# Expert stage of a state-space and mixture-of-experts layer: all gathers ahead of all scatters, rows kept in place, four weight buffers

## What is computed

```
gate = softmax(xr @ Wg); idx = argmax(gate); g = gate[idx]
loc  = rank of the token among those of its expert;  valid = loc < 256
dispatched[idx, loc] = xr                        # 16 x 256 x 128
h = relu(dispatched @ w1[e])                     # 256 x 128 @ 128 x 512
expert_out = h @ w2[e]                           # 256 x 512 @ 512 x 128
out = x + expert_out[idx, loc] * g * valid
```

## Time and profile before

| | |
|---|---|
| median of three runs | 721.25 us (720.04 to 721.40) |
| the profiled execution | span 721.6 us, 12778 instructions |
| TensorE products busy | 613.1 us, 85% |
| TensorE weight loads busy | 478.9 us, 66% |
| VectorE busy | 557.2 us, 77% |
| ScalarE busy | 527.8 us, 73% |
| GpSimd busy | 591.7 us, 82% |
| data moved | 85.20 MB, mean 118 GB/s |
| first gather starts | 616.30 us |
| last scatter's instruction ends | 716.10 us |

### The profile page before, as it was taken

One profiled execution on the slowest core, in us unless ns is written; L12 is line 12 of the kernel. 1 busy time (PEld: TensorE's weight loads), 2 busy tenths in 40 slices (PEclk: granted clock), 3 DMA queues, 4 the chain that ended last, 5 costly groups with the idle time before them and its releaser, 6 DMA issues.

```text
span 721.6 us, 12778 instructions
## 1 busy us (share of the span) xinstructions
PE 613.1 (85%) x4034; PEld 478.9 (66%) x4034; DVE 557.2 (77%) x892; ACT 527.8 (73%) x1043; POOL 591.7 (82%) x411
## 2 busy tenths in 40 slices
PE   5689989989989898998989999899878881987593
PEld 3336677757767776776767667676777761876483
DVE  5558899999999999999999999999987876222131
ACT  3699989899989989998999999899786320132130
POOL 5268999999999999999999999998997830656754
PEclk9989999999999999999999999999968895789897
DMA  4241533245145334524534442262343013345451
GB/s 138 82 149 62 155 111 131 86 129 170 64 150 164 127 106 121 157 84 128 180 110 133 105 171 77 75 207 84 115 127 113 23 42 98 88 149 163 122 176 50
DMA packets 60752, 85.20 MB, mean 118 GB/s; under 512 B 14321, under 2 KB 40214, under 8 KB 60686
## 3 DMA queue, kind: packets, MB, share of 16 engines
q1 hardware_dynamic: 57176, 78.05, 34.8%
q0 software_dynamic: 2560, 6.08, 2.8%
q10 hardware_dynamic: 950, 0.27, 0.2%
HBM read 72.27 MB, written 12.32 MB: 117 GB/s over the span
## 4 chain that ended last, share of the span: by engine, by line
POOL 55%; issue 21%; PE 13%; another core or an unknown queue 3%; DVE 3%; ACT 1%; DMA 1%; POOLq 1%; SPq 0%; DVEq 0%; ACTq 0%
POOL h L888 27%; POOL h L902 18%; PE ps L622 3%; POOL u L875 3%; PE ps L635 3%; POOL cs L913 2%; POOL fac L918 2%; PE ps L1676 1%; PE ps L1792 1%; POOL lnp L849 1%; POOL rstd L925 1%; PE ps L642 1%; PE ps L602 1%; PE ps L610 1%
## 5 line engine op out<-in xcount | busy, mean ns | idle before, releaser
L1413 DVE TENSOR_TENSOR_SCAN h<-ps,h 128x902 f32<-128x902 f32 x204 | 319.8, 1608 | 24.6 <-ACT ps L1029 16.5
L888 POOL TENSOR_TENSOR h<-u,scr 128x1280 f32<-128x1280 f32 x104 | 283.4, 2742 | 2.9
L1792 PEld LDWEIGHTS ps<-h,ident 128*128 128x128 f32 x1632 | 233.6, 196 | 22.9 <-issue 19.1
L1792 PE MATMUL ps<-h,ident 128*128 128x160 f32 x1632 | 239.9, 307 | 3.4 <-issue 3.4
L1139 ACT ACTIVATE z<-dtb,asc 128x240 f32<-128x240 f32 (+3 forms) x432 | 201.6, 537 | 0.1
L1029 ACT ACTIVATE ps<-z 128x820 f32<-128x820 f32 (+1 forms) x208 | 137.8, 687 | 35.5 <-DVE h L1413 28.9
L902 POOL TENSOR_TENSOR h<-h,scr 128x1280 f32<-128x1280 f32 (+1 forms) x52 | 138.0, 2654 | 0.7 <-DVE h L1429 0.7
L1464 DVE TENSOR_TENSOR h<-h,ps 128x640 f32<-128x640 f32 (+1 forms) x155 | 87.8, 577 | 0.2
L1676 PE MATMUL ps<-xnT,wT 128*128 128x488 f32 x144 | 73.9, 626 | 0.0
L1039 ACT ACTIVATE sqb<-h 128x208 f32<-128x208 f32 x102 | 44.8, 441 | 24.8 <-DVE h L1413 22.0
L398 POOL DMA_INDIRECT z<-rows_d,gidx x32 | 33.0, 1032 | 34.6 <-DVE gidx L532 25.2
(11 more groups left out here) (200 smaller groups left out, 801.4 us busy)
## 6 DMA issues: line engine op xcount, KB each, us to landing
scr<-b_d SPq DMA_DIRECT2D x52, 640.0 KB, 4.8
scr<-c_d SPq DMA_DIRECT2D x52, 320.0 KB, 4.9
z<-in_L_ffn_w_dram SPq DMA_DIRECT2D x32, 256.0 KB
cdg<-cdg_d SPq DMA_DIRECT2D x52, 60.0 KB
xx_d<-xx SPq DMA_DIRECT2D x8, 256.0 KB, 2.0
xxr<-xx_d SPq DMA_DIRECT2D x8, 256.0 KB, 2.8
rows_d<-h2b SPq DMA_DIRECT2D x16, 120.0 KB, 2.1
rows_d<-xxr SPq DMA_DIRECT2D x16, 120.0 KB, 2.3
```

The source lines that it names most:

```text
L888: pool.tensor_tensor(hr[:, hf * RH:(hf + 1) * RH, 1:SLOT].rearrange("p (n b) t -> p n b t", b=B), us.unsqueeze(1).to_broadcast([P, NST, B, ...
L1413: dve.tensor_tensor_scan(hs, region(G)[:, 0:(r1 - r0) * SLOT], hs, 0.0, ALU.mult, ALU.add).then_inc(gscan, 1)
L1792: pe.matmul(ps[:, YB, 0:H * BS], ident[:], hr[:, :, n * B:(n + 1) * B, 0:SEG], start=(n == 0), stop=False)
```

## The change

- `xs` has a place for each of the 16 experts, so no gather waits for a place. All 32 gathers are issued first, then all 32 scatters, each pair after its `fin_made`.
- `xin`, `xxe` and `fin` are gone, and with them `take_in` and `keep_xx` on ScalarE. TensorE turns the normed half straight from `xs`, after the gather. `take_out` reads the residual half of `xs`, writes its result over it, and the scatter reads it there. VectorE waits for the gather in place of `xxe_ready`, and no more for scatters.
- w1 and w2 have four places each. Four experts are loaded at the start; then w1 of e + 4 after the up products of e, w2 of e + 4 after the down products of e.
- To make room in `z`, the tiles `ohhi`, `idw`, `gtw` and `xTs` move from `z` into the area of `h`.
- The gathers have a semaphore for each expert, the scatters one for all. The loops over the experts are plain ones with the same order on TensorE and VectorE.

The diff, cut to its core:

```diff
-        w1s, o = take(z, o, 2, F)
-        w2s, o = take(z, o, 2, FC, DM)
-        xin, o = take(z, o, 2, CT, DM)
+        xs, o = take(z, o, E, CT, 2 * DM)
+        w1s, o = take(z, o, WR, F)
+        w2s, o = take(z, o, WR, FC, DM)
...
+        hTs, o = take(hf_, 0, 2, FC, CAP)
+        xTs, o = take(hf_, o, 2, CAP)
+        ohhi, o = take(hf_, o, NT * NS // 2)
...
-        xs, o = take(z, o, WR, CT, 2 * DM)
-        fin, o = take(z, o, WR, CT, DM)
-        xxe, o = take(z, o, WR, CT, DM)
-        AHEAD = 7
...
-            load_w1(0, 0)
-            load_w2(0, 0)
-            load_w1(1, 1)
-            load_w2(1, 1)
-
-            for e in range(E - 1):
-                if e + 2 < E:
-                    sp.wait_ge(up_done, 2 * (e + 1))
-                    load_w1(e + 2, e % 2)
-                if e > 0:
-                    sp.wait_ge(down_done, e)
-                    load_w2(e + 1, (e + 1) % 2)
-            for q in range(WR):
-                sp.wait_ge(scattered[q], 16 * CT * (E // WR))
+            for e in range(WR):
+                load_w1(e, e)
+                load_w2(e, e)
+            for e in range(E - WR):
+                sp.wait_ge(up_done, 2 * (e + 1))
+                load_w1(e + WR, e % WR)
+                sp.wait_ge(down_done, e + 1)
+                load_w2(e + WR, e % WR)
+            sp.wait_ge(scattered, 16 * NS)
...
             def gather(e):
 
-                at_least(pool, xin_ready, e - WR + 1)
-                at_least(pool, xxe_ready, e - WR + 1)
                 for t in range(CT):
                     i = CT * e + t
-                    pool.indirect_dma_start(xs[:, e % WR, t, :], None, rows_d,
+                    pool.indirect_dma_start(xs[:, e, t, :], None, rows_d,
...
-                                            fin[:, e % WR, t, :], None,
+                                            xs[:, e, t, DM:2 * DM], None,
...
             pool.wait_ge(idx_ready, 1)
-            for e in range(AHEAD):
+            for e in range(E):
                 gather(e)
             pool.wait_ge(idx_ready, 2)
             for e in range(E):
                 pool.wait_ge(fin_made, e + 1)
                 scatter(e)
-                if e + AHEAD < E:
-                    gather(e + AHEAD)
...
-            def keep_xx(e, k):
...
-            def take_in(e, k, loads):
...
+            for e in range(1, E):
+                turn_in(e, e % 2)
+                relu(e - 1, (e - 1) % 2)
+            relu(E - 1, (E - 1) % 2)
...
-            def take_out(e, k, before):
+            def take_out(e):
 
                 dve.wait_ge(down_done, e + 1)
-                dve.wait_ge(xxe_ready, e + 1)
-                at_least(dve, scattered[k], 16 * CT * before)
+                dve.wait_ge(gathered[e], 16 * CT)
                 for t in range(CT):
-                    ins = dve.scalar_tensor_tensor(out=fin[:, k, t, :], in0=ps[:, 6 + k % 2, t * P:(t + 1) * P],
-                                                   scalar=gs[:, bass.ds(CT * e + t, 1)], in1=xxe[:, k, t, :],
+                    kept = xs[:, e, t, DM:2 * DM]
+                    ins = dve.scalar_tensor_tensor(out=kept, in0=ps[:, 6 + e % 2, t * P:(t + 1) * P],
+                                                   scalar=gs[:, CT * e + t:CT * e + t + 1], in1=kept,
                                                    op0=ALU.mult, op1=ALU.add)
...
             def turn(e, k):
-                pe.wait_ge(xin_ready, e + 1)
+                pe.wait_ge(gathered[e], 16 * CT)
                 at_least(pe, xeT_ready, e - 1)
                 for t in range(CT):
-                    ins = pe.transpose(ps[:, k, t * P:(t + 1) * P], xin[:, k, t, :], ident[:])
+                    ins = pe.transpose(ps[:, k, t * P:(t + 1) * P], xs[:, e, t, 0:DM], ident[:])
```

More of the change, by code:

```diff
@@ L352, in mamba_moe @@
         ld_lg = sem("ld_lg")
[L353 to L357, removed]
+        ld_w1 = [sem(f"ld_w1{k}") for k in range(WR)]
+        ld_w2 = [sem(f"ld_w2{k}") for k in range(WR)]
+        iol_ready = sem("iol_ready"); full_ready = sem("full_ready")
+        gathered = [sem(f"gathered{k}") for k in range(E)]
+        scattered = sem("scattered")
         rt = sem("rt"); em_ready = sem("em_ready"); ex_done = sem("ex_done")
@@ L364, in mamba_moe @@
         relu_a = sem("relu_a"); relu_b = sem("relu_b"); down_done = sem("down_done")
-        fin_made = sem("fin_made"); xxe_ready = sem("xxe_ready")
+        fin_made = sem("fin_made")
         def sp_tail(sp):
@@ L438, in relu @@
                                ACT.Relu).then_inc(relu_a, 1)
-            def keep_xx(e, k):
-                at_least(act, fin_made, e - WR + 1)
-                act.copy(xxe[:, k], xs[:, k, :, DM:2 * DM]).then_inc(xxe_ready, 1)
-            def take_in(e, k, loads):
[L447 to L451, removed]
-            turn_in(0, 0)
[L453 to L472, removed]
+            turn_in(0, 0)
+            for e in range(1, E):
+                turn_in(e, e % 2)
+                relu(e - 1, (e - 1) % 2)
+            relu(E - 1, (E - 1) % 2)
         def route_step(dve, n):
@@ L567, in dve_tail @@
             dve.wait_ge(gs_ready, 1)
-            take_out(0, 0, 0)
+            take_out(0)
             relu(1, 1)
[L570 to L574, removed]
-            take_out(3, 3, 0)
-            relu(5, 1)
-            for g in range(1, E // WR - 1):
-                for k in range(WR):
-                    take_out(WR * g + k, k, g)
-                    relu(WR * g + k + 2, k % 2)
-            for e in range(E - WR, E):
-                take_out(e, e % WR, E // WR - 1)
-                if e + 2 < E:
-                    relu(e + 2, e % 2)
+            for e in range(1, E):
+                if e + 1 < E:
+                    relu(e + 1, (e + 1) % 2)
+                take_out(e)
         def pe_tail(pe):
@@ L622, in up, with down @@
                     ins = pe.matmul(ps[:, 2 + 2 * q + c // 2, (c % 2) * CAP:(c % 2 + 1) * CAP],
-                                    w1s[:, k, c * P:(c + 1) * P], xTs[:, q, :], start=True, stop=True)
+                                    w1s[:, e % WR, c * P:(c + 1) * P], xTs[:, q, :], start=True, stop=True)
                     if c % 2:
                         ins.then_inc(up_done, 1)
-            def down(e, k, loads):
+            def down(e, k):
                 q = k
-                pe.wait_ge(ld_w2[k], 16 * loads)
+                pe.wait_ge(ld_w2[e % WR], 16 * (e // WR + 1))
                 pe.wait_ge(relu_a, e + 1)
@@ L635, in down @@
                         ins = pe.matmul(ps[:, 6 + q, t * P:(t + 1) * P], hTs[:, q, c, t * P:(t + 1) * P],
-                                        w2s[:, k, c, :], start=(c == 0), stop=(c == FC - 1))
+                                        w2s[:, e % WR, c, :], start=(c == 0), stop=(c == FC - 1))
                 ins.then_inc(down_done, 1)
@@ L643, in pe_tail @@
             turn(0, 0)
-            up(0, 0, 1)
+            up(0, 0)
             turn(1, 1)
@@ L647, in pe_tail @@
             pe.wait_ge(idx_ready, 2)
-            down(0, 0, 1)
-            up(1, 1, 1)
+            down(0, 0)
+            up(1, 1)
             turn(2, 0)
             pe.wait_ge(gs_ready, 1)
-            for g in range(1, E // 2 - 1):
-                turn(2 * g + 1, 1)
-                up(2 * g, 0, g + 1)
-                down(2 * g - 1, 1, g)
-                turn(2 * g + 2, 0)
-                up(2 * g + 1, 1, g + 1)
-                down(2 * g, 0, g + 1)
-            turn(E - 1, 1)
-            up(E - 2, 0, E // 2)
-            down(E - 3, 1, E // 2 - 1)
-            up(E - 1, 1, E // 2)
-            down(E - 2, 0, E // 2)
-            down(E - 1, 1, E // 2)
+            for e in range(2, E):
+                if e + 1 < E:
+                    turn(e + 1, (e + 1) % 2)
+                up(e, e % 2)
+                down(e - 1, (e - 1) % 2)
+            down(E - 1, (E - 1) % 2)
         block = ctx.enter_context(nc.Block())
```

15 lines of the change are left out of this document (6 added, 9 removed).

## The result

The changed kernel took 725.38 us (median of 8 runs, 723.89 to 727.81) against 721.52 us for the kernel before (8 runs, 720.04 to 724.35): a ratio of 1.0056, 95% interval 1.004 to 1.0071. It is **slower by 0.6%**. The forecast was 716.4 us, the range 706 to 724.

The account below looks back on a forecast made before the run. GpSimd's transfer queue and late TensorE completions were taken to bound the tail; from 721.6 us, -6.5 for the earlier last result, +1.7 for the clock and -0.35 for the median gave 716.4 us, range 706 to 724.

Parts of the forecast that it names:

- The reading of the bound: Expert tail: GpSimd's queue (64 x 1.30 = 83 us) and late TensorE completions, turned into idle time by engine waits.
- the held phase: While GpSimd issues on after expert 0 (told at 636.5), experts finish every 5.7 us, until expert 7 at 676.4.
- H: Lateness with which TensorE's completions reach other engines while GpSimd issues without a break; taken as 5 us.
- the looser chain: Expert stage without ScalarE's copies: TensorE's turn waits for the gather alone; pace 5.7 us an expert, formerly 7.9.
- fixed rate: Rival: completions pass at 7.9 us an expert while GpSimd issues, whatever waits for them; 719.4 us, chance 0.26.
- The copies as a link: Two ScalarE copies an expert: worth nothing as busy time, but their removal shortens the pace from H + 2.95 to H + 0.7.
- The slower rival: Lateness grows with the run of 32 gathers, so no expert is finished in them; 723.9 us at full price, chance 0.20.
- the point of decision: In the slower case, whether expert 2's down products are told after 664.2; put at 665.1, 0.9 late.
- The queue bound: Rival: completions hardly delay the chain, so GpSimd's queue of transfers ends the kernel at 705.0 us; chance 0.20 below 711.
- The clock term: TensorE runs at half rate after a stall, slowing one up and down pair; 1.7 us added once.
- The density of 2.6 us in 3.73: Once scatters catch up with results, GpSimd's work for each expert leaves TensorE running free at 3.73 us an expert.
- Taking 0.35 off: Last step of the sum: from the profiled span of 721.6 to the runs' median of 721.25 us.

Follow-up runs that it names:

- e7: Changed kernel with one pause: GpSimd waits for expert 0's result before gathering expert 7; 725.65 us on chip 5, 1.0042 of the kernel before.
- e8: Changed kernel with only GpSimd's order set back (seven experts gathered ahead, then scatters and gathers in turn); 722.51 us on chip 5, 0.9992 of the kernel before.

## Why the prediction was wrong

**The reading of the bound** held. Late completions and GpSimd's queue were the two things, and both are now shown by runs: with the plain loads in place of the indirect gathers the kernel ends 21 to 26 us earlier on late chips and 7 to 9 on the prompt one. The difference of the two, some 14 to 17 us, is what lateness costs.

**The step that failed is "the held phase".** I took the lateness as a delay H of 5 us that the looser chain would mostly ride over: 5.7 us an expert, expert 7 done at 676.4. Measured: expert 0 told at 639.6, 25.2 us after the first gather where before had 20.3; expert 1 23.7 us after it. The lateness is no fixed delay and no fixed rate. It is larger the longer the run of indirect transfers goes on without a pause: 2.8 us for the gates (630.4), 9.0 for the down products of expert 0 (639.7), 18.4 for the up products of expert 1 (650.8), 22.4 and 26.4 for the two turns (655.0 and 659.2). The statement that expert 0 is told at 636.5 "for the same 14 gathers run ahead of it" was wrong in itself: it is freed by the pause after them, as e7 shows, and the change takes the pause away.

**The copies as a link** (H + 2.95 against H + 0.7) were worth nothing: e8, with everything but the order, stands at 0.9992 on a late chip. The formula had been fitted to one stretch of 24 us with one free number.

**The slower rival** had the mechanism right (the lateness grows with the run, GpSimd runs out of results to scatter) and the point of decision: what counts is whether expert 2 is told before 664.2. It was told at 665.78, which is 3.4 us too late once the first gather's 1.8 us are put back. Where it was wrong is in what frees TensorE: in this trace the turn of expert 2 was told at 655.0, while GpSimd still issued; on chip 5 the pause did free it. Its price, +2.6 us, has to be held against the first gather: the last result came 3.2 us later than before, relative to it. On chip 5 the loss was 9.0 us, since there TensorE ran again only at 663.1 and 665.7; I had no term for how much the hold differs between chips. The range's high end, 724, was 1.4 us short of the median.

**The queue bound** was computed right, 64 starts at 1.30 us; it decides on prompt chips, where 706.06 us were measured. **The clock term** was there but too small: the restart's up and down took 3.75 and 2.80 us, 2.7 us over, where the sum had 1.7. **The density of 2.6 us in 3.73** held: from 665 on no completion is over 1 us late. Four weight places, results in place and moved tiles cost nothing that e8 shows.

**Time and span.** I called the span of 721.6 us the profiled execution's own time, 0.35 us above the median. A time is 1.7 to 1.8 us above its span in every run here, so that execution took some 723.4 us (an estimate), 2 us above the median. Taking 0.35 off still gave the number meant, the median of before less 4.8 us, so this step did not make the miss.

The rule of the Trainium skill (Perfetto Trace Analysis, Tensor Engine Instruction) that a product's recorded end is computed and its semaphore comes after PSUM's acknowledgement is in keeping with recorded ends that precede their effect by up to 26 us. What holds the completion these runs do not show.

## What to carry to other kernels

Where GpSimd issues indirect transfers beside TensorE work, look at the gap between a product's recorded end and its consumer's start before moving anything: on two of the three chips identified here long unpaused runs of them delayed TensorE's completions. Six gathers out did no harm, ten or eleven made a completion 1.5 to 2.8 us late, and 34 in a row stalled TensorE for 23 to 31 us. The batch that looks better for the queue was 0.6% worse in the first comparison, 1.1 to 1.3% worse on chip 5 and 0.3% better on chip 15. Leave pauses in such runs where TensorE's results are waited for, but expect little where the queue itself is nearly the bound: no paused order here beat the kernel before by more than 0.2%. If the rows allow it, load by plain transfers (21 to 26 us on late chips, 7 to 9 on the prompt one). Compare two kernels on one chip, and on more than one chip, before a fraction of a percent is believed.

## What the runs showed of the hardware that was not expected

- The same kernel takes 707 us on chip 15 and 721 to 723 us on chips 5 and 1, and with plain loads in place of the gathers 697 to 700 us on all three. The difference is late completions of TensorE beside indirect transfers of GpSimd.
- On the late chips gathers and scatters alike do it, 1 KB and 512-byte rows alike (stalls of 30.8 us on chip 5 and 26.5 on chip 1). Plain transfers of the same size by SP (at 262 GB/s) or by GpSimd do not.
- In a long run not only completions come late: products start singly, 1.4 us apart (e7).
- Two transfers in each 3.73 us leave TensorE all but untouched for 40 us. What in an indirect transfer holds a completion, and why a chip does it or not, stays open: neither the number of rows in a transfer nor the length of a pause was varied by itself, and no indirect transfer with its rows in order was tried.
